# The two closing norms of an encoder: shift and scale as columns after a turn, or as rows before it

## What is computed

```python
def _ln(h, g, b, eps=1e-05):
    m = h.mean(-1, keepdims=True)
    v = h.var(-1, keepdims=True)
    return (h - m) * jax.lax.rsqrt(v + eps) * g + b
...
def layer(h, p):
    ...                                        # attention, 16 heads of 8
    h = _ln(h + att, g1, be1)
    ff = jax.nn.gelu(h @ w1 + b1_, approximate=False) @ w2 + b2_
    h = _ln(h + ff, g2, be2)
    return (h, None)
h, _ = jax.lax.scan(layer, h, params)          # six layers
return _ln(h, lnf_g, lnf_b)
...
x = _layernorm(x + _L0_attn_ref(x, ...), axis=-1)   # _layernorm has no gain and no bias
x = _layernorm(x + _L0_ffn_ref(x, ...), axis=-1)    # the next stage: experts
```

## Time and profile before

| | us |
|---|---|
| median of 3 executions | 4078.39 (4074.07 to 4080.16) |
| profiled execution, its own time | 4066.18 |
| its span in the profile | 4064.3 |
| PE busy / weight loads | 3361.5 / 2346.5 |
| VectorE, ScalarE, POOL busy | 2516.9, 1836.2, 1057.6 |
| mean granted clock of TensorE | 0.904 of full speed |

### The profile page before, as it was taken

One profiled execution on the slowest core, in us unless ns is written; L12 is line 12 of the kernel. 1 busy time (PEld: TensorE's weight loads), 2 busy tenths in 40 slices (PEclk: granted clock), 3 DMA queues, 4 the chain that ended last, 5 costly groups with the idle time before them and its releaser, 6 DMA issues. The chain is left out here.

```text
span 4064.3 us, 68321 instructions
## 1 busy us (share of the span) xinstructions
PE 3361.5 (83%) x25711; PEld 2346.5 (58%) x25711; DVE 2516.9 (62%) x6468; ACT 1836.2 (45%) x3001; POOL 1057.6 (26%) x1362
## 2 busy tenths in 40 slices
PE   5999999999999999997769586777566659997996
PEld 3666666666666666665568254556344434444664
DVE  5866865875775875874511598886686651115663
ACT  2565565565565565565434553222232123332453
POOL 2324324324324324322454210000200320004221
PEclk8999999999999999999789777999776769997997
DMA  5524524434433533530145100000000000004430
GB/s 135 123 66 101 121 67 99 117 73 99 114 77 93 118 79 91 117 78 22 53 149 186 50 1 1 1 1 1 5 0 29 0 11 0 0 0 97 102 82 22
DMA packets 177020, 262.06 MB, mean 64 GB/s; under 512 B 19950, under 2 KB 149230, under 8 KB 159694
## 3 DMA queue, kind: packets, MB, share of 16 engines
q1 hardware_dynamic: 152494, 140.93, 12.4%
q10 hardware_dynamic: 19656, 107.37, 12.0%
q0 software_dynamic: 4544, 9.38, 0.7%
HBM read 184.67 MB, written 72.19 MB: 63 GB/s over the span
## 5 line engine op out<-in xcount | busy, mean ns | idle before, releaser
L870 DVE TENSOR_REDUCE enc_mx<-psum 128x2 f32<-128x512 f32 (+1 forms) x1152 | 755.6, 685 | 154.2 <-PE psum L550 151.5
L1036 ACT ACTIVATE enc_e<-psum 128x1024 f32<-128x1024 f32 (+1 forms) x768 | 580.3, 808 | 397.1 <-PE psum L571 303.5
L550 PE MATMUL psum<-enc_ks,enc_qs 80*128 80x128 bf16 (+1 forms) x3072 | 459.4, 254 | 69.0 <-DVE enc_mx L870 55.2
L571 PE MATMUL psum<-enc_qs,enc_ks 83*128 83x256 bf16 (+1 forms) x3072 | 379.3, 248 | 27.3 <-DMA enc_qs<-enc_turned_max 19.1
L550 PEld LDWEIGHTS psum<-enc_ks,enc_qs 80*128 80x128 bf16 x3072 | 222.3, 100 | 189.4 <-DVE enc_mx L870 109.5
L584 PE MATMUL psum<-enc_e,enc_v 128*32 128x256 f32 (+1 forms) x6144 | 331.0, 333 | 0.0
L571 PEld LDWEIGHTS psum<-enc_qs,enc_ks 83*128 83x128 bf16 x3072 | 257.8, 98 | 65.0 <-DMA enc_qs<-enc_turned_max 19.6
L584 PEld LDWEIGHTS psum<-enc_e,enc_v 128*32 128x32 f32 x6144 | 160.8, 109 | 160.8 <-ACT enc_e L1036 52.3
L2781 PE MATMUL psum<-ter_h,weights_b 128*128 128x512 f32 x512 | 224.9, 593 | 2.4 <-DVE ter_h L2832 1.6
L640 PE MATMUL psum<-par_layerr,enc_hidden 128*128 128x128 f32 x1536 | 193.9, 281 | 16.2 <-DVE enc_n_rows L915 16.2
L640 PEld LDWEIGHTS psum<-par_layerr,enc_hidden 128*128 128x128 f32 x1536 | 184.8, 196 | 27.0 <-DVE enc_n_rows L915 21.2
(11 more groups left out here) (531 smaller groups left out, 7234.5 us busy)
## 6 DMA issues: line engine op xcount, KB each, us to landing
enc_qs<-q_pieces ACTq DMA_DIRECT2D x234, 192.0 KB
enc_ks<-k_pieces ACTq DMA_DIRECT2D x234, 192.0 KB
k_pieces<-enc_pieces SPq DMA_DIRECT2D x240, 128.0 KB, 2.0
moe_wb<-moe_w SPq DMA_DIRECT2D x39, 512.0 KB, 4.1
q_pieces<-enc_pieces SPq DMA_DIRECT2D x144, 128.0 KB, 2.1
enc_qs<-q_pieces SPq DMA_DIRECT2D x54, 192.0 KB
enc_ks<-k_pieces SPq DMA_DIRECT2D x54, 192.0 KB
rope_qs<-q_pieces ACTq DMA_DIRECT2D x39, 192.0 KB
```

What stands on the lines that cost most here:

```text
L550: last = T_.matmul(p1[f % 2][:, i * kw:(i + 1) * kw], qs[0:KEYED, slot, h, j * P:(j + 1) * P], ks[0:KEYED, slot, h, 0:kw], start=True, sto ...
L571: last = T_.matmul(p2[ch][:, g], ks[0:SCORED, slot, 4 * T + g, ch * P:(ch + 1) * P], qs[0:SCORED, slot, 4 * T + g, 0:n], start=True, stop= ...
L870: V.tensor_reduce(mx[:, u % 2, j * HEADS + h0:j * HEADS + h0 + n], p1[f % 2].rearrange("p (h k) -> p h k", h=n), AX_X, ALU.max)\
L1036: A.activation(e_of(T, ch), p2[ch], ACT.Exp, scale=HD ** -0.5).then_inc(s_e, 1)
```

## The change

The final norm's gain and bias, the layer's own gain and bias, and x are all kept as rows: the same 128 numbers on every partition, so that they can be used while tokens lie on the partitions. Then the whole path from N2 to N4 stays in that layout:

- POOL multiplies N2's normed rows by the gain `g2r` and adds `be2r` (into `N3.rows`), and adds the final norm's bias `bfr` to x in place.
- N3 and N4 become pair chains: statistics, power and offset as for N2, applied on ScalarE.
- VectorE multiplies N3's normed rows by `gfr` and adds x (into `N4.rows`).
- PE turns N4 once per group, into the banks 5 and 1 in turn, and ScalarE copies the turn to H.

`back2` and `turn_rows` of the last layer, `rows_of`, `inner` and `both` are gone. x is loaded from a new tensor that holds it by rows, of the same size; the stage's first load `par_s` carries `gfr` and `bfr`, 256 columns in place of 2. The last layer's loop issues one round fewer on VectorE, PE and POOL.

```diff
-    def apply(self, act, n):
+    def apply(self, act, n, read=None, times=None):
         act.wait_ge(self.s_offset, n + 1)
         if n >= 2:
-            act.wait_ge(self.s_turned, n - 1)
+            act.wait_ge(read or self.s_turned, n - 1 if times is None else times)
...
-        N4 = Chain(c, sb, sem, "n4_", tiled(spare(2)), tiled(spare(3)))
-        inner, both = spare(4), spare(5)
+        x0 = ks[:].rearrange("p a h q -> p (a h q)")[:, 0:2 * TOKENS].bitcast(F32).rearrange("p (g t d) -> p g t d", g=GROUPS, t=TILES)
+        pair = lambda i: qs[:].rearrange("p a h q -> p (a h q)")[:, 4 * i * GROUP:4 * (i + 1) * GROUP].bitcast(F32).rearrange("p (n t d) -> p n t d", n=2, t=TILES)
+        N3 = PairChain(c, sb, sem, "n3_", pair(0), pair(1))
+        N4 = PairChain(c, sb, sem, "n4_", pair(2), pair(3))
+        along = lambda row: row.unsqueeze(1).broadcast_to([P, TILES, D])
         grp = lambda g: slice(g * GROUP, (g + 1) * GROUP)
         zero = W["zero"].rearrange("p (c q) -> p c q", c=JT)
         e_of = lambda T, ch: (e[:, T % 2, 0:HT * S].rearrange("p (g q) -> p g q", g=4), e[:, T % 2, HT * S:].rearrange("p (g q) -> p g q", g=4))[ch]
...
             def close(k):
                 if 0 <= k - 2 < GROUPS:
                     N3.root(pool, k - 2)
-                if 0 <= k - 4 < GROUPS:
-                    N4.root(pool, k - 4)
+                    N3.centre(pool, k - 2)
                 if 0 <= k - 3 < GROUPS:
-                    g = k - 3
+                    N4.root(pool, k - 3)
+                    N4.centre(pool, k - 3)
+                if 0 <= k - 1 < GROUPS:
+                    g = k - 1
+                    n = GROUPS * (LAYERS - 1) + g
                     if g == 0:
                         pool.wait_ge(s_x0, 16)
-                    else:
-                        pool.wait_ge(N4.s_rows, g)
-                    pool.wait_ge(s_inner, g + 1)
-                    G.tensor_tensor(both, inner, x0[:, grp(g)], ALU.add).then_inc(s_sum, 1)
+                    pool.wait_ge(N2.s_normed, n + 1)
+                    if g >= 2:
+                        pool.wait_ge(N3.s_normed, g - 1)
+                    G.tensor_tensor(N3.rows[:, g % 2], N2.normed[:, n % 2], along(LR["g2r"]), ALU.mult).then_inc(s_z, 1)
+                    pool.wait_ge(s_z, g + 1)
+                    G.tensor_tensor(N3.rows[:, g % 2], N3.rows[:, g % 2], along(LR["be2r"]), ALU.add).then_inc(N3.s_moved, 1)
+                    G.tensor_tensor(x0[:, g], x0[:, g], along(W["bfr"]), ALU.add).then_inc(s_x0b, 1)
 
             def attend(layer, last):
                 for u in range(SEQS):
...
-                    last = T_.transpose(b[:, t * P:(t + 1) * P], src[:, t * P:(t + 1) * P], c.ident)
-                last.then_inc(chain.s_rows, 1)
-
             def close(k):
-
-                if 0 <= k - 2 < GROUPS:
-                    g = k - 2
-                    pe.wait_ge(N2.s_done, GROUPS * LAYERS + g + 1)
+                if 0 <= k - 4 < GROUPS:
+                    g = k - 4
                     if g == 0:
                         pe.wait_ge(N1.s_done, GROUPS * LAYERS)
-                    if g >= 3:
-                        pe.wait_ge(N4.s_moved, g - 2)
-                    rows_of(N3, c.H[:, grp(g)], bank[0])
-                if 0 <= k - 3 < GROUPS:
-                    g = k - 3
-                    if g >= 3:
-                        pe.wait_ge(N4.s_done, g - 2)
-                    N3.turn(pe, g, bank[1])
-                if 0 <= k - 4 < GROUPS:
-                    g = k - 4
-                    pe.wait_ge(s_sum, g + 1)
-                    pe.wait_ge(N3.s_moved, min(g + 3, GROUPS))
-                    if g + 2 >= GROUPS:
-                        pe.wait_ge(N4.s_moved, g)
-                    rows_of(N4, both, bank[0])
-                if 0 <= k - 5 < GROUPS:
-                    g = k - 5
-                    pe.wait_ge(s_inner, min(g + 3, GROUPS))
-                    if g + 2 >= GROUPS:
-                        pe.wait_ge(N4.s_done, g)
-                    N4.turn(pe, g, bank[1])
+                    if g >= 2:
+                        pe.wait_ge(N4.s_done, g - 1)
+                    N4.turn(pe, g, (misc, bank[1])[g % 2])
 
             def last_turn(layer, b):
                 N2.turn(pe, at(layer, GROUPS, GROUPS - 1), b)
...
@@ -789,8 +770,6 @@
                         pe.wait_ge(s_rest, at(layer, 2 * GROUPS, 3, 1))
                         project_v(layer, 1, 0, bank[0])
                     down(layer, g, lambda t: among(g, t))
-                    if g and last_layer:
-                        turn_rows(g - 1)
                     if g == 2 and not last_layer:
                         pe.wait_ge(N1.s_moved, at(layer, GROUPS, GROUPS))
                         for w in range(2):
...
                         fill(layer, 1, 1, f)
                 if last_layer:
-                    pe.wait_ge(N2.s_done, at(layer, GROUPS, 2 * GROUPS - 1))
-                    last_turn(layer, misc)
-                    for k in range(GROUPS, GROUPS + 5):
+                    for k in range(GROUPS, GROUPS + 4):
                         close(k)
 
...
             def close(k):
                 if 0 <= k - 2 < GROUPS:
                     N3.statistics(dve, k - 2)
-                if 0 <= k - 4 < GROUPS:
-                    N4.statistics(dve, k - 4)
-                if 0 <= k - 2 < GROUPS:
-                    if k - 2:
-                        dve.wait_ge(N3.s_turned, k - 2)
-                    N3.apply(dve, k - 2)
-                if 0 <= k - 4 < GROUPS:
-                    if k - 4:
-                        dve.wait_ge(N4.s_turned, k - 4)
-                    N4.apply(dve, k - 4)
+                if 0 <= k - 3 < GROUPS:
+                    g = k - 3
+                    dve.wait_ge(N3.s_normed, g + 1)
+                    if g >= 2:
+                        dve.wait_ge(N4.s_normed, g - 1)
+                    V.tensor_tensor(N4.rows[:, g % 2], N3.normed[:, g % 2], along(W["gfr"]), ALU.mult).then_inc(s_w, 1)
+                    dve.wait_ge(s_w, g + 1)
+                    dve.wait_ge(s_x0b, g + 1)
+                    V.tensor_tensor(N4.rows[:, g % 2], N4.rows[:, g % 2], x0[:, g], ALU.add).then_inc(N4.s_moved, 1)
+                    N4.statistics(dve, g)
 
             def attend(layer, last):
                 for u in range(SEQS):
...
                 n = at(layer, GROUPS, g)
-                if n >= 2:
-                    act.wait_ge(s_scaled2, min(n - 1, layer * GROUPS) if last else n - 1)
-                N2.apply(act, n)
+                if last and g >= 2:
+                    N2.apply(act, n, s_z, g - 1)
+                elif n >= 2:
+                    act.wait_ge(s_scaled2, n - 1)
+                    N2.apply(act, n)
+                else:
+                    N2.apply(act, n)
 
             def back2(layer, g, b):
                 N2.back(act, at(layer, GROUPS, g), b, grp(g), LR["g2"], LR["be2"])
 
             def close(k):
                 if 0 <= k - 2 < GROUPS:
-                    if k - 2:
-                        act.wait_ge(N3.s_normed, k - 2)
-                    N3.move(act, k - 2, bank[0])
+                    N3.apply(act, k - 2, s_w)
                 if 0 <= k - 3 < GROUPS:
-                    g = k - 3
-                    act.wait_ge(N3.s_turned, g + 1)
-                    if g:
-                        act.wait_ge(s_sum, g)
-                    A.activation(inner, bank[1], ACT.Identity, bias=W["bf"], scale=W["gf"]).then_inc(s_inner, 1)
-                if 0 <= k - 4 < GROUPS:
-                    if k - 4:
-                        act.wait_ge(N4.s_normed, k - 4)
-                    N4.move(act, k - 4, bank[0])
+                    N4.apply(act, k - 3)
                 if 0 <= k - 5 < GROUPS:
                     g = k - 5
                     act.wait_ge(N4.s_turned, g + 1)
-                    A.activation(c.H[:, grp(g)], bank[1], ACT.Copy).then_inc(N4.s_done, 1)
+                    A.activation(c.H[:, grp(g)], (misc, bank[1])[g % 2], ACT.Copy).then_inc(N4.s_done, 1)
 
             def attend(layer, last):
                 for u in range(SEQS):
...
     col = lambda a: a.reshape(-1, P).T
     g = lambda n: inp["L0_attn_" + n]
-    out["s1"] = {"zero": zero, "pos": pos.T, "gf": col(g("lnf_g")), "bf": col(g("lnf_b")),
+    out["s1"] = {"zero": zero, "pos": pos.T, "gfr": np.broadcast_to(g("lnf_g"), (P, D)), "bfr": np.broadcast_to(g("lnf_b"), (P, D)),
...
@@ -3801,6 +3769,7 @@
         return nc.dram_tensor(name, a.shape, _mybir.dt.from_np(a.dtype), kind="ExternalInput").ap()
 
     x_t = dram("x_t", inp["L0_attn_x"].reshape(TOKENS, D).T)
+    params["x_rows"] = dram("x_rows", inp["L0_attn_x"].reshape(GROUPS * TILES, P, D).transpose(1, 0, 2).reshape(P, -1))
     layers = {"layerq": [], "layerr": []}
```

More of the change, by code:

```diff
@@ L198, with __init__ @@
 class PairChain:
[L201 removed]
+    def __init__(self, c, sb, sem, tag, rows=None, normed=None):
         self.c = c
[L203 removed]
```

(8 more changed lines are left out.)

13 lines of the change are left out of this document (2 added, 11 removed).

## The result

| | before | after |
|---|---|---|
| median, us | 4079.27 (4074.07 to 4080.9, 4 executions) | 4036.16 (4033.11 to 4040.42, 4 executions) |
| ratio | | 0.9904, 95% interval 0.9891 to 0.9917 |
| profiled execution, its own time | 4066.18 | 4040.42 |
| its span | 4064.3 | 4038.6 |
| PE, VectorE, ScalarE, POOL busy | 3361.5, 2516.9, 1836.2, 1057.6 | 3341.6, 2508.9, 1837.6, 1083.2 |

The change saves 43.1 us between the medians; the interval allows 33.9 to 44.5. The forecast was 4040, range 4028 to 4056.

The account below looks back on a forecast made before the run. Waits bound the last layer's feed-forward and closing norms, a baton of 13.6 us a turn. Gains of 11.9, 19.8 and 7.6 less 0.6 at the start, 38.7 net off 4078.4, gave about 4040 us, range 4028 to 4056.

Parts of the forecast that it names:

- What bounded it: Last layer's feed-forward and closing norms: no engine full; a baton of steps, each waiting for the one before, 13.57 us a turn.
- The new turn of 8.5: Last layer's loop: POOL's and VectorE's orders lock into one round summing to 8.5 us; other engines' work fits beside it.
- The lead-in: Up to add2(3): group 2's second linear layer ends 0.4 us earlier, add2(3) at 1862.0 against 1873.91; gain 11.9 us.
- residual1 at 2.0: POOL's two late passes for the last attention group stand in the four turns' chain: 2.0 us added.
- turns of 9.5 or more: Sign, in the last layer's loop, that the prediction would be wrong; turns of 8.5 us were expected.
- The tail at 25.2: From add2(7) to the end of the last copy to H: 25.2 us against 32.8, gain 7.6.
- The start at 0.6: Stage's first load grows by 127 KB, delaying VectorE's first pass and perhaps PE's first product: cost 0.6 us, bounds 0 and 1.0.
- Colliding passes: Rival: VectorE's scale or add waits under a POOL pass in the loop; worst case 13 us, 4053; chance 10%.
- ScalarE: Rival: ScalarE bounds the loop, its gelus fed slowly by PE; turn 9.5 us, time 4046; chance 12%.
- The clock: Rival: PE granted half clock in the loop, its 7.5 us become 15; only the tail gains, 4070; chance 4%.
- Slower through the experts: Rival: PE stays at low clock in the expert stage over 47 us longer, eating the gain; 4087 at 55; chance 3%.
- Sum: Lead-in 11.9, four turns 19.8 and tail 7.6 make 39.3 us; less 0.6 at the start, net gain 38.7.

Follow-up runs that it names:

- pair_only: Kernel before, with N3 and N4 as pair chains applied on ScalarE, all five transpose sets kept: 0.9985 of the time before; gelu load to last copy 125.75 us.
- layout_only: Changed kernel, but N3 and N4 applied on VectorE without offsets: 0.9953 of the time before; gelu load to last copy 116.6 us.
- more_vector: Changed kernel with VectorE's scale by the final gain done twice a turn: turn 9.19 us, gelu load to last copy 102.0 us.
- more_pool: Changed kernel with a fourth wide pass on POOL each round, into an unread buffer: turn 9.40 us, gelu load to last copy 105.2 us.
- more_scalar: Changed kernel with two extra 128x512 copies a turn on ScalarE: turn 8.44 us, gelu load to last copy 96.9 us.
- more_tensor: Changed kernel with 16 extra transposes a turn on PE from turn 3 on: turn 8.44 us, gelu load to last copy 97.0 us.
- hold_passes: Changed kernel with POOL's group 0 passes held until VectorE applied the last attention norm: gelu load to last copy 95.6 us; 4046.25 us, one execution.
- split_residual: Changed kernel, x shifted early, residual1's two passes put singly behind two turns' shifts: gelu load to last copy 94.75 us; 4033.39 us, one execution.
- three_together: Changed kernel with POOL's group 0 passes held, residual1's passes split behind shifts, POOL and ScalarE reordered in the tail: gelu load to last copy 90.4 us; 4037.12 us.
- after_again: The changed kernel unchanged, run once more: 4035.35 us; gelu load to last copy 96.9 us.

## Why the prediction held, and where it was off

- **What bounded it**: right. pair_only and layout_only keep half of the baton each, and their turns are 12.0 and 12.3 us in the mean. One reading was off and cost nothing: ScalarE loses four moves out of PSUM and keeps the fifth, where the prediction says that it loses five and keeps one.
- **The new turn of 8.5**: right, 8.45, by the steps worked out. Power to offset 1.08, to the scale 0.15, scale 1.35, shift 1.30, N3's statistics 1.47, scale 0.72, add 0.73, and N4's statistics to POOL's next power 1.65 (1875.38 to 1877.03), together 8.45. The margin of 0.25 us between POOL's third pass and VectorE's scale was 0.26 (1882.12 to 1882.38). more_vector and more_pool show that it is these two engines, more_scalar and more_tensor that it is not the others in this loop.
- **The lead-in**: 33.3 us after the gelu load was forecast, 35.07 measured. The failed step is that the second linear layer of group 2 "would end 0.4 earlier". Counted from the gelu load it ended at 27.14 instead of 26.17, a microsecond later, because down(2) waited for add2(1), which VectorE reached 2.9 late while four applies of N1 stood under POOL's new passes. The rule for this stood in the prediction (a wide pass on POOL holds such an instruction back); it was used on the steady turn alone. In hold_passes down(2) ends at 25.73, 0.4 earlier as forecast, and 1.3 of the 1.7 come back. The other 0.4 lies behind it: add2(3) stood behind VectorE's own work and not behind PE, whose down(3) had ended 0.5 before.
- **residual1 at 2.0**: 2.2, and only because of its place (split_residual). The working given, 2.6 less 0.9, makes 1.7 and not 2.0; POOL idles 0.39 in an undisturbed turn, and 2.6 less 0.4 is the 2.2 measured. It also came as two turns of 9.5 and not as one of 10.5, since its pass held L225 and so add2. By the letter, "turns of 9.5 or more" was the prediction's own sign of being wrong; split_residual shows that these two are residual1's and that the steady turn is 8.45.
- **The tail at 25.2**: 25.9. N3's last power took 1.39 us in place of 1.01, beside VectorE's scale and add of the group before: 0.4 of the 0.7. The rest is PE's last turn, which started 2.18 us after ScalarE's last apply instead of the 1.8 forecast: it waited for a copy to H that stood behind that apply on ScalarE and freed its bank. With the copy ahead, in three_together, it is 1.79.
- **The start at 0.6**: no cost seen. The load of 592 KB landed in 3.7 and 3.8 us (after, after_again), against 3.5 and 3.3 for 465 KB, so its 127 KB cost 0.2 to 0.5 and not the 1.0 of a rate. VectorE's first pass began at 13.16 and 13.57 instead of 13.02 and 12.93, but PE's first product at 26.30 and 26.17, against 26.48 and 28.91 before.
- **Rivals.** *Colliding passes*: L902 and L905 never collided in the changed kernel, so the turn didn't pay; but small instructions did, which the rival hadn't named. *ScalarE*: it waits 1.4 us or more for POOL's offset in each of the four turns, and more_scalar clears it. *The clock*: as said, see the rows below; down(7) took 6.24 us after PE had waited 4.55, which cost nothing, since add2(7) came after 8.44. *Slower through the experts*: what lies behind the stretch took 2108.4 and 2103.9 us after, 2101.8 and 2103.8 before; nothing like the 47 us that rival needed. The experts' first product came 6.0 and 6.2 us behind the last copy and not some 5 (5.3 before), because the next stage's load took 4.6 and 4.9 us instead of 3.9 and 4.0. Over all runs it took 3.9 to 4.9; whether the change has a part in that stays open.
- **Sum**: 38.7 forecast net, 36.9 in the stretch with nothing at the start. Taken off the median shown, 36.9 gives 4041.5; the measured 4036.2 is lower by some 5 us that the stretch doesn't show, so the closeness of 4040 is partly luck.

The clock, in the table of stretches after (the three numbers at the end are PEclk, DMA share, GB/s):

```profile
1868.40:1894.00 25.60, 22.33 (x131) 16.07 (x129) 19.28 (x99) 20.23 (x46) 24.10 (x27) 1.00 0.00 1
1894.00:1904.36 10.36, 6.68 (x36) 6.44 (x36) 8.63 (x48) 6.62 (x17) 9.37 (x12) 0.67 0.00 0
```

and PE's timeline there:

```profile
1896.66 6.24 PE L646 MATMUL psum<-par_layerr,enc_hidden 128*128 128x128 f32 x32 [4.55 <-DVE enc_n_rows L892]
```

Up to 1894 PE was granted the full 2.4 GHz; before the wait of 4.55 us its longest one in that stretch was 0.88. Behind it the mean was 0.67, between the levels of 2.4 and 1.2 GHz.

## What to carry over

A loop of engines that release each other is as long as the instructions in its round, and what a pass costs depends on its place: the same two passes cost 2.2 us ahead of the release and nothing in two places behind it that other work had left. Work added there without making room cost 0.96. Look for collisions where the new loop overlaps the old work, at its entry and exit, and among the small instructions, not only in its steady turn. Two changes can be worth more together than their sum (8.1 and 17.2 alone, 36.9 together): here the new layout brings the passes under which VectorE's applies are held, and the other half moves these applies to ScalarE.

## What was not expected of the hardware

- **Small instructions are held too.** VectorE's 128x4 tensor_scalar (L224, L225), 0.17 us alone, took 0.67 at 1878.90 and 1.24 at 1885.23 under POOL's wide passes, 1.13 in more_pool; each ended within 0.1 of POOL's pass. The statistics of four 128x128 tiles (L216) kept their 0.87 beside the same passes.
- **It goes the other way too.** POOL's offset, 0.20 us alone, took 0.69 while VectorE added x; POOL's timeline after:

```profile
1874.71 0.69 POOL L233 TENSOR_TENSOR enc_n_offset<-enc_n_minus,enc_n_rstd 128x4 f32<-128x4 f32 x1
```

and VectorE's:

```profile
1874.65 0.69 DVE L905 TENSOR_TENSOR enc_qs<-enc_qs,enc_ks 128x512 f32<-128x512 f32 x1
```

VectorE's had started 0.06 earlier, and the offset ended 0.06 after it. The Trainium skill, "SBUF — State Buffer", section "Who interferes with whom", says that tensor_scalar can take the shared pair and that "issue order, not op shape, decides who blocks"; both directions in this trace agree.

- **POOL's power didn't hold VectorE.** VectorE's scale at 1882.38 started 0.3 us into a power of 1.02 us on POOL (L229 at 1882.07) and took its 0.68, as L897 took its 0.29. The other way a power is held: the one at 1918.49 started under VectorE's scale and took 1.39.
